# Block 1 of a one-layer transformer on one core: GpSimd rounds the gated values' high halves in block 0's FFN, six of eight pairs of block 1's attention go by fp16 halves, and VectorE makes its last ten q stacks

## The reference

```python
h = _L0_tok_ref(x, emb_table, norm_weight, proj_weight)      # rms_norm, einsum, rms_norm
h = h + _L0_attn_ref(_layernorm(h), wq, wk, wv, wo)
h = h + _L0_ffn_ref(_layernorm(h), w_gate, w_up, w_down)
# attention: q, k, v = x @ wq, x @ wk, x @ wv; softmax(q k^T / 4 + causal mask) v; @ wo
# ffn: (silu(x @ w_gate.T) * (x @ w_up.T)) @ w_down.T
```

## Time and profile before

| | |
|---|---|
| median of 3 runs | 717.11 us (717.09 to 717.43) |
| the profiled execution's own time | 717.22 us |
| its span | 715.5 us |
| PE busy | 688.6 us, 96% of the span |
| DVE, ACT, POOL busy | 410.2, 333.4 and 313.4 us |
| mean granted TensorE clock | 0.986 of full speed |

### The profile page before, as it was taken

One profiled execution on the slowest core, in us unless ns is written; L12 is line 12 of the kernel. 1 busy time (PEld: TensorE's weight loads), 2 busy tenths in 40 slices (PEclk: granted clock), 3 DMA queues, 4 the chain that ended last, 5 costly groups with the idle time before them and its releaser, 6 DMA issues.

```text
span 715.5 us, 16315 instructions
## 1 busy us (share of the span) xinstructions
PE 688.6 (96%) x6399; PEld 525.3 (73%) x6399; DVE 410.2 (57%) x1019; ACT 333.4 (47%) x676; POOL 313.4 (44%) x410
## 2 busy tenths in 40 slices
PE   8459999999999999999999999999999999999998
PEld 5359688965997479866996589856996599747873
DVE  7767789886655465545656365445655465543320
ACT  6426377861665146621664156522663166512320
POOL 5020315761565436751675336552665256511220
PEclk9859999999999999999999999999999999999999
DMA  8759500011000110012000300011000200000000
GB/s 316 288 206 404 191 18 1 3 47 61 17 2 2 60 63 1 2 47 77 2 1 2 106 17 2 1 61 62 2 2 16 93 16 2 1 16 16 2 1 29
DMA packets 10459, 40.37 MB, mean 56 GB/s; under 512 B 1808, under 2 KB 2576, under 8 KB 8592
## 3 DMA queue, kind: packets, MB, share of 16 engines
q1 hardware_dynamic: 6912, 25.44, 9.1%
q0 software_dynamic: 3328, 13.11, 5.9%
q10 hardware_dynamic: 144, 0.79, 0.3%
HBM read 29.89 MB, written 9.44 MB: 55 GB/s over the span
## 4 chain that ended last, share of the span: by engine, by line
PE 80%; DVE 10%; ACT 5%; issue 2%; DMA 1%; SPq 0%; ACTq 0%; DVEq 0%
PE banks L1120 13%; PE banks L1125 13%; PE banks L1121 13%; PE banks L1226 6%; PE banks L1228 6%; PE banks L1227 6%; PE banks L1073 3%; PE banks L1091 2%; PE banks L1167 2%; PE banks L1062 2%; PE banks L1173 2%; PE banks L1168 2%; DVE gate_work L831 2%; DVE ffn_weights L786 1%; PE banks L1053 1%
## 5 line engine op out<-in xcount | busy, mean ns | idle before, releaser
L1121 PE MATMUL banks<-xnT_and_h,ffn_weights 128*128 128x256 f16 x1024 | 237.3, 272 | 0.0
L1120 PE MATMUL banks<-xnT_and_h,ffn_weights 128*128 128x256 f16 x1024 | 237.2, 272 | 0.0
L390 POOL TENSOR_TENSOR gated_split<-gate_work,gated_split 128x256 f16<-128x256 f32 x128 | 88.4, 691 | 243.0 <-ACT gated_split L533 243.0
L1125 PE MATMUL banks<-xnT_and_h,ffn_weights 128*128 128x256 f16 x1024 | 153.6, 273 | 0.0
L394 POOL TENSOR_TENSOR weights_split<-weights,weights_split 128x512 f16<-128x512 f32 x104 | 123.2, 1185 | 0.0
L1120 PEld LDWEIGHTS banks<-xnT_and_h,ffn_weights 128*128 128x128 f16 x1024 | 100.4, 98 | 11.4
L1125 PEld LDWEIGHTS banks<-xnT_and_h,ffn_weights 128*128 128x128 f16 x1024 | 100.2, 98 | 11.6
L1121 PEld LDWEIGHTS banks<-xnT_and_h,ffn_weights 128*128 128x128 f16 x1024 | 99.9, 98 | 11.4
L521 ACT ACTIVATE gate_work<-banks,scales 128x256 f32<-128x256 f32 x128 | 60.6, 474 | 99.1 <-PE banks L1125 99.1
L529 ACT ACTIVATE weights<-banks,scales 128x512 f32<-128x512 f32 x128 | 87.3, 682 | 14.0 <-PE banks L1073 14.0
L843 DVE SCALAR_TENSOR_TENSOR weights<-weights,counts_T 128x512 f32<-128x512 f32 x128 | 87.6, 685 | 9.1 <-ACT weights L529 9.0
(11 more groups left out here) (236 smaller groups left out, 1043.4 us busy)
## 6 DMA issues: line engine op xcount, KB each, us to landing
ffn_weights<-in_ffn_w SPq DMA_DIRECT2D x12, 1024.0 KB, 9.9
out_rows_dram<-ffn_weights SPq DMA_DIRECT2D x16, 256.0 KB, 2.0
xnT_and_h<-in_wqkv SPq DMA_DIRECT2D x1, 1536.0 KB, 8.7
local_table<-gated_split SPq DMA_DIRECT2D x2, 640.0 KB, 5.3
local_table<-xnT_and_h SPq DMA_DIRECT2D x2, 640.0 KB, 5.8
gated_split<-in_projT SPq DMA_DIRECT2D x4, 256.0 KB, 4.3
ffn_weights<-in_wo SPq DMA_DIRECT2D x1, 1024.0 KB, 10.7
token_table<-weights_split ACTq DMA_DIRECT2D x1, 768.0 KB, 6.0
```

The source lines that it names most:

```text
L390: g.tensor_tensor(gtl[:, j, :], g2[j % 2], gth[:, j, :], ALU.subtract).then_inc(gt_lo, 1)
L1120: t.matmul(o, wh, xTh[m % 2][:, c, :], start=c == 0, stop=False)
L1121: t.matmul(o, wl, xTh[m % 2][:, c, :], start=False, stop=False)
L1125: last = t.matmul(o, gu_w(s, up, c, 0), xTl[m % 2][:, c, :], start=False, stop=c == DC - 1)
```

## The change

It has three parts, all in phase 1 (attention of block 1, FFN of block 0):

1. `gth` of block 0 is made by POOL with a copy (a cast from float32 to fp16) instead of by ACT. POOL waits for g2 by itself now.
2. Pairs 12 and 14 go by halves too, so that only pairs 8 and 10 are wide. `TAIL_PAIRS` shrinks to pair 9: pairs 11 and 13 go back to the usual bank.
3. The q stacks of units 22 to 31 are made by DVE instead of ACT (slots 5 to 14).

```diff
-HALF_PAIRS = (9, 11, 13, 15)
-TAIL_PAIRS = (9, 11, 13)
+HALF_PAIRS = (9, 11, 12, 13, 14, 15)
+TAIL_PAIRS = (9,)
+DVE_STACK = UPB + 6
...
                     if ffn and 1 <= s <= HC:
                         j = s - 1
                         i = m * HC + j
+                        if m == 0:
+                            pool.wait_ge(g2_rdy, i + 1)
+                            g.tensor_copy(gth[:, j, :], g2[j % 2]).then_inc(gt_hi, 1)
                         pool.wait_ge(gt_hi, i + 1)
                         g.tensor_tensor(gtl[:, j, :], g2[j % 2], gth[:, j, :], ALU.subtract).then_inc(gt_lo, 1)
...
-                    if att and n <= 1 and s + 1 < UPB:
+                    if att and s + 1 < UPB and n * UPB + s + 1 < DVE_STACK:
                         stack(n * UPB + s + 1)
...
-                    if ffn and 1 <= s <= HC:
+                    if ffn and m > 0 and 1 <= s <= HC:
                         j = s - 1
                         actq.wait_ge(g2_rdy, m * HC + j + 1)
+                        if m == 1 and j == 0:
+                            actq.wait_ge(gt_hi, HC)
                         a.activation(gth[:, j, :], g2[j % 2], ACT.Copy).then_inc(gt_hi, 1)
...
-                    if att and n > 1 and s + 1 < UPB:
+                    if att and s + 1 < UPB and n * UPB + s + 1 >= DVE_STACK:
                         stack(n * UPB + s + 1)
```

## The result

The changed kernel takes 720.66 us (719.62 to 720.86, 5 runs) against 717.11 us (716.7 to 717.43, 5 runs): 1.0047 times as long, 95% interval 1.0032 to 1.0061, or 3.4 us. The forecast was 718.4 with a range up to 720.4. The mechanism forecast is there, but the time is 2.3 us above it.

The account below looks back on a forecast made before the run. PE was taken to set the time, DVE and ACT close behind; after the change, POOL's and DVE's turns. wo at 150.7 instead of 149.44 gave 717.22 + 1.3 = 718.5 us profiled, 718.4 median; range 714.3 to 720.4.

Parts of the forecast that it names:

- 2.7 us off PE: Phase 1, pairs 12 and 14: four units by halves instead of wide, 0.67 us each, take 2.7 us off PE.
- ACT has time in hand: Slots 0 to 15 of phase 1: ACT's busy time falls from 48.1 to 41 us of 58.
- the move of pairs 11 and 13 costs nothing: Phase 1: back in the usual bank at no cost, since `values` opens a slot or more after the previous pair's eviction.
- POOL and DVE exclude each other: Phase 1: two-SBUF-input DVE operations and POOL's do not overlap; one stands until the other has all but ended.
- rival C: Phase 1: POOL doesn't hold up DVE's count product, 0.55 us less per slot, 3.35 per slot; 715.4 us, chance 0.18.
- D: POOL's cast is dear: at 0.67 us it adds 0.27 in each of eight slots; 720.6 us, chance 0.14.
- B: PE's saving of 2.7 us comes through, perhaps with half of its 1.7 of waits: 714.4 to 713.6 us, chance 0.20.
- 3.9 us per slot: Slots 8 to 15 of phase 1: turns of POOL and DVE set the pace at 3.9 us, against PE's 3.16.
- Slot 15 at 147.7: DVE, phase 1: from slot 9 at 124.6 us, six slots at 3.8 to 3.9 bring slot 15 to 147.7.
- 2.8 us from there to unit 29's low half at 150.5: Slot 15: stack or first product, g2, rest of a `gtl`, count product and `WTl` take some 2.8 us.
- Slots 1 to 6 a gain of 0.1: PE up to slot 7: some waits for ACT's stacks go, gaining 0.1 us (0 to 1.0).
- No further loss behind slot 16: After phase 1's slot 16: POOL catches up by about 159 us, later phases unchanged, so +1.3 us stays.

Follow-up runs that it names:

- the chunk's turn short: Changed kernel with low halves of weight chunks 4 to 23 made by a one-SBUF-input VectorE operation, subtraction left out: 713.3 us (0.9949 against the kernel before).
- PE kept busy: Changed kernel with 10 and 19 unread matmuls ahead of the values product in slots 6 and 14 of phase 1: 720.84 us (1.0057 against the kernel before).

## Why the prediction was wrong

- **What bounds the kernel now, and 2.7 us off PE:** right. With the chunk's turn short, the kernel comes to 55.0 us to wo, 3.6 less than before: 2.7 for the units and most of the 1.3 of waits.
- **ACT has time in hand, and the move of pairs 11 and 13 costs nothing:** the sum of busy time was right, the conclusion wrong as a general step. In the changed kernel PE's waits in slots 0 to 15 are all for POOL behind slot 5, and the runs suggest that this is because the cast left ACT. With gth on ACT the evictions come behind its wait for g2, and PE waits 2.0 us (with stacks on DVE) or 3.4 us (without). Lengthening the bank list took these waits away and gained nothing to wo, since other waits took their place, for POOL's low half and in slot 15 and at wo.
- **POOL and DVE exclude each other, POOL's idle time is paid by DVE:** right, also for the count product behind POOL (1.01 for 0.68 at 133.86), so that rival C falls; and the cast took 0.40, so that D falls. B falls too.
- **3.9 us per slot:** right. With the clock kept up, slot 9 of DVE began 33.9 us after `gate_up(0)` (I had 124.6 - 90.85 = 33.75) and slot 15 at 57.35 (I had 56.85), which is 3.9 per slot. In the changed kernel itself the six slots took 3.86 each, from 35.55 to the end of slot 14's chunk at 58.7. Slots 7 and 8 took 6.5 us together against my 6.6.
- **Slot 15 at 147.7, and 2.8 us from there to unit 29's low half at 150.5:** this is the step that failed. With the clock kept up that low half ended 61.9 us after `gate_up(0)` instead of 59.65, 2.3 us late. Half a microsecond is slot 15 beginning late: in slot 14 the count product waited 0.84 us for ACT's exp, which had waited 1.84 for the low half of unit 27, one of the waits for three buffers, and my walk had none. The other 1.8 us are the last step, which took 4.6 us and not 2.8. DVE from the start of slot 15, then POOL, in the kernel with PE kept busy:

```profile
148.60 0.41 DVE L837 SCALAR_TENSOR_TENSOR gate_work<-gate_work,banks 128x256 f32<-128x256 f32 x1
...
149.38 0.68 DVE L849 SCALAR_TENSOR_TENSOR weights<-weights,counts_T 128x512 f32<-128x512 f32 x1
...
150.72 1.43 DVE L792 SCALAR_TENSOR_TENSOR ffn_weights<-ffn_weights,scales 128x1024 f16<-128x1024 f32 x1
```

```profile
149.43 0.90 POOL L392 CAST gated_split<-gate_work 128x256 f16<-128x256 f32 x1
150.40 0.67 POOL L394 TENSOR_TENSOR gated_split<-gate_work,gated_split 128x256 f16<-128x256 f32 x1
151.03 2.14 POOL L398 TENSOR_TENSOR weights_split<-weights,weights_split 128x512 f16<-128x512 f32 x1
```

  I took the cast as done and left only 0.2 us of a `gtl`, and I let the unit's low half go ahead of the slot's chunk. In the trace POOL is still at y of a pair until 149.5, so cast and `gtl` come whole behind it (the cast behind the count product), and then the chunk takes its turn first: the low half of 1.16 us takes 2.14. So the price of the turns was right, and where POOL stood in them at the end was wrong. In the changed kernel itself the low half ended at 61.7 us, and PE, held up by the clock, came to it only just ahead of wo at 63.2. The low halves of units 22 to 29 ended 4.27 us apart on average (29.9 us in all), more than a slot of DVE, since POOL had just waited for DVE in the slot of unit 22 and stood well behind it in that of unit 29.
- **Slots 1 to 6 a gain of 0.1:** small miss. `gate_up(6)` began 0.2 later than before, not earlier.
- **The clock:** missing from the forecast. I forecast 4 us of waits of PE for POOL and did not ask what such a wait does to the granted clock; the rows of before, all at 1.00, gave no price for it. In the profiled executions it is the rest of what is missing to wo, 1.05 us. In device time it did not show: 720.84 with PE kept busy against 720.66, which itself comes from an execution at a mean clock of 0.986.
- **No further loss behind slot 16:** right, 565.8 us against 566.0.

So of +4.65 us to wo in the profiled execution, +1.3 were forecast, 2.3 are the end of the walk (0.5 and 1.8) and 1.05 the clock. The medians are 2.3 us apart from the forecast, which the end of the walk fills by itself. What stays open is why the clock falls behind some of PE's waits and not behind others like them, and whether VectorE's count product or a form of `split_low` with truly one port would be free of POOL: neither was separated.

## What to carry to other kernels

An idle engine is not free capacity if its operations exclude those of an engine that is close to the bound: add up the turns of both, not the busy time of each, and look for the same operation with two durations in the trace. Look also at what one engine's late work (here ACT's evictions behind a wait for g2) hides: cast and pairs cost 0.9 and 1.9 us to wo alone and 5.4 together. Add up queues to the very operation that the next engine waits for, with what stands ahead of it there: the pace of the turns was forecast right here, and their end was not. The order of two operations within a slot was worth about 2 us of device time in the changed kernel with the work unchanged, more than any of the three parts gained.

## What the runs showed of the hardware

- In the profiled execution of the changed kernel the granted clock halved for 3.4 us after PE had mostly waited for 1.7 us (slot 6, beginning 1.7 us after PE was busy again) and for 2.15 us (slot 14, beginning at once). It did not fall behind the same 1.66 us in the kernel without the pairs, behind 2.15 us in the kernel without the stacks, or behind 1.4 us in slot 6 of before (0.67 us busy in 111.92 to 113.35). With the waits filled by matmuls whose results nobody reads it did not fall either.
- Two falls cost PE 1.65 us each. In the profiled executions 1.05 of the 3.3 us showed at wo, and in device time nothing that can be told from the spread.
- Turns of VectorE's and GpSimd's operations stand inside the instructions: the same `split_low` took 1.27 us alone and 2.06 to 2.18 behind a unit's low half, the count product 0.68 alone and 1.01 behind a running `gtl`.
- A GpSimd cast of 128x256 from float32 to fp16 took 0.40 us alone, 1.39 behind VectorE's 128x1024 operation, and the `gtl` behind it started 0.08 us after its end.
